# Gated cross-attention with two experts' stages: the first batch's front of the second attention is ordered ahead of the second batch's

## The chip, the cores and the metric

One Trainium2 chip, one core (core 0). The metric is device time in microseconds from the first to the last instruction of one execution, as the chip's clock counts it. Other cores are idle. TensorE, VectorE, ScalarE and GpSimd each run their own instruction stream in order; SyncE issues transfers (SP below), and 16 DMA engines carry them. Engines wait for each other by semaphores only.

## The reference, cut to what matters

Four stages add to a residual x of 8 batches x 256 tokens x 512: an attention with rotary positions, an expert stage, a second attention with normed queries and keys, and a routed stage of sparse maps. Only the second attention is touched:

```python
q = _ln((x @ Wq + bq).reshape(b, s1, H, HD), qn_w, qn_b)            # 16 heads of 32
kv = jnp.concatenate([y_main @ Wk + bk, y_main @ Wv + bv], axis=-1)
kv = kv.reshape(b, s2, H, 2 * HD)
k = _ln(kv[..., :HD], kn_w, kn_b)
v = kv[..., HD:]
ctx = _attn(qT, k.transpose(0, 2, 1, 3), v.transpose(0, 2, 1, 3))
ctx_dca = _attn(qT, k_dca.transpose(0, 2, 1, 3), v_dca.transpose(0, 2, 1, 3))  # last 16 rows
ctx = ctx + DCA_WEIGHT * ctx_dca
return ctx @ Wo + bo
```

Here `_ln` is a layer norm over the 32 columns of one head, with a weight and a bias, and x is itself layer-normed over its 512 columns before it comes in. The context y has 256 rows per batch, of which the last 16 have weights of their own and a softmax of their own.

## The kernel before, in words

`normed_attention` computes this stage. A batch is 256 tokens, two tiles of 128. Heads are worked in pairs: 8 pairs per batch, 64 steps in all. In step s, TensorE turns the exponentials of pair s (line 2221) and computes the scores of pair s + 2 (`scores`, line 2211); VectorE takes the maxima of pair s + 1 (`top`, 1925), ScalarE its exponentials (2039), GpSimd scales its last 16 columns (`second_scaled`, 1849 to 1853).

The front of a batch makes what the pairs need. It is a list of named items, and the table `ITEMS_AT` gives the step of each, counted from the batch's own first pair (batch b starts at step 8b): C turns the context, X0 and X1 turn the normed tokens, Q0, Q1, K1, K0 are the products whose results are normed per head, V1 and V0 the values. Each Q or K tile is evacuated by ScalarE into `cen` (2087), squared by GpSimd (`squares`, 1828), summed per head by VectorE (1951). When all four are summed, VectorE takes the inverse square roots of 64 sums per row in a chain of 13 small operations (`over_spread`, 1959 and 84 to 97; called the spread below). Then GpSimd norms the tile in three operations (`norm`, 1836, 1839, 1842), ScalarE makes the high part (2096), VectorE the low part (1966), and items q0a, q1a, k1a, k0a (first four pairs) and q0b, q1b, k1b, k0b (last four) turn them on TensorE (2145). ScalarE evacuates the units of tile 0, VectorE those of tile 1, both into `qT` and `kT`, and SP copies these into the layout of the scores, `q4` in 4 transfers and `k4` in 8 (`spread_out`, 1747 and 1752). Three PSUM banks `W` are used in turn by all items.

Other tables place the rest: `SQUARED_AT`, `SUMMED_AT`, `SPREAD`, `SCALED_AT`, `HIGH_AT`, `LOW_AT` and `TOKENS` (GpSimd applies the layer norm to x, 1820). Statistics of x: those of batch 0 and 1 are taken before the loop; those of batches 2 to 7 (12 tiles) at the steps of `STATS_AT` (2012), and at step `SCALES` a chain of 20 small operations turns them into scales (`layer_norm_scalars`, 113 to 127). GpSimd's tokens of batch 2 wait for that (`all_scales`).

Each engine walks the steps from `FIRST` to `LAST` and in each step issues what the tables name for every batch. So the fronts of batch 0 and batch 1 overlap before step 0: batch 0's items stand at steps -17 to 0, batch 1's at -9 to 8. DCA items D, E, F make the 16 rows once, and SP puts them into `cen` and V of each batch (`dca_keys` 1758, `dca_values` 1763).

## Time and profile before

| | us |
|---|---|
| median of 3 runs | 2203.88 |
| lowest, highest | 2186.25, 2235.4 |
| the profiled execution | 2186.77 |
| its span, first to last instruction | 2185.0 |
| TensorE busy in the span | 1893.5 |
| VectorE, ScalarE, GpSimd busy | 1127.2, 921.9, 1012.6 |

The rows of the trace that matter have a section of their own. A row of the timeline gives the start in us from the span's start, the length, the engine, the line of the program, the operation, output <- input, how many were merged, and in brackets the idle time of the engine before it and who ended that. The second attention begins near 1462 us; its pair loop ends near 1898 us.

### The profile page before, as it was taken

To read this page: it belongs to the slowest core of one execution; us is meant where nothing else is said; L and a number is where in the kernel's file an instruction comes from. 1 tells how busy PE (TensorE), PEld (TensorE's weight loads), DVE (VectorE), ACT (ScalarE), POOL (GpSimd) and SP (SyncE) were. 2 spreads that over 40 slices of the span, in tenths; PEclk is the share of its full clock that TensorE was granted. 3 is DMA by queue.
4 is the path that set the end of the run, shared out by engine and by line. 5 is a ranking of instruction groups with operands and counts; after the bars stand their busy time and mean duration, and the time that the engine had idled before them with its cause. 6 is when DMAs were issued, how large, how long until landed. Compare 5 with 4: busy or idle time off the path is not lost. (4 is left out here: it accounts for less than half of the span.)

```text
span 2185.0 us, 37999 instructions
## 1 busy us (share of the span) xinstructions
PE 1893.5 (87%) x11294; PEld 1380.0 (63%) x11294; DVE 1127.2 (52%) x2563; ACT 921.9 (42%) x2626; POOL 1012.6 (46%) x1058
## 2 busy tenths in 40 slices
PE   4689999999879999989999999966799999765992
PEld 1355666666549899978888899953565655422441
DVE  5567767777545763322332222226677778561114
ACT  3367777776633322222222222212566666432110
POOL 1478777877510542222333343424565454155540
PEclk9999999999889999999999999988899999977996
DMA  8588888787715663579778766432444444182446
GB/s 313 179 250 261 262 250 247 227 254 237 239 48 180 113 140 87 149 216 283 210 198 233 228 163 161 88 74 85 96 99 98 92 100 110 33 231 77 138 135 259
DMA packets 189404, 373.74 MB, mean 171 GB/s; under 512 B 47658, under 2 KB 89267, under 8 KB 183380
## 3 DMA queue, kind: packets, MB, share of 16 engines
q1 hardware_dynamic: 157596, 309.18, 46.6%
q0 software_dynamic: 31616, 62.14, 13.3%
q8 instruction: 104, 1.70, 0.3%
q14 instruction: 88, 0.72, 0.1%
HBM read 193.42 MB, written 135.33 MB: 150 GB/s over the span
## 5 line engine op out<-in xcount | busy, mean ns | idle before, releaser
L701 ACT ACTIVATE a_P<-a_SC,a_nm 128x256 f32<-128x256 f32 x512 | 235.9, 473 | 132.2 <-DVE a_nm L606 131.4
L1174 POOL DMA_INDIRECT b_y_rows<-b_ysb,b_entry x79 | 124.6, 1577 | 351.2 <-DMA b_y_rows<-b_ysb,b_entry 227.4
L606 DVE TENSOR_REDUCE a_nm<-a_SC 128x2 f32<-128x512 f32 x256 | 164.8, 685 | 142.4 <-PE a_SC L847 142.4
L1383 DVE TENSOR_TENSOR b_xl<-b_XT,b_xh 128x512 fp32r<-128x512 f32 x111 | 76.7, 691 | 250.0 <-ACT b_xh L1325 248.9
L569 POOL TENSOR_TENSOR a_praw<-a_praw,a_phigh 128x704 f32<-128x704 f32 (+2 forms) x126 | 191.2, 1517 | 10.3
L858 PEld LDWEIGHTS a_T<-ident,a_P 128*128 128x128 f32 x1024 | 119.2, 145 | 74.6 <-issue 39.7
L858 PE MATMUL a_T<-ident,a_P 128*128 128x128 f32 x1024 | 147.2, 283 | 21.5 <-DVE a_PT L618 20.6
L567 POOL CAST a_phigh<-a_praw 128x704 fp32r<-128x704 f32 (+2 forms) x126 | 112.7, 895 | 93.8 <-DMA a_praw<-in_L_ffn_wd 32.6
L1389 DVE TENSOR_TENSOR b_al<-b_AT,b_ah 128x384 fp32r<-128x384 f32 x111 | 61.8, 557 | 176.7 <-ACT b_ah L1330 176.7
L1320 ACT ACTIVATE b_ysb<-b_Y 128x512 f32<-128x512 f32 x79 | 47.3, 598 | 249.5 <-PE b_Y L1265 249.5
L2039 ACT ACTIVATE c_P<-c_SC,c_nm 128x240 f32<-128x240 f32 x256 | 115.7, 457 | 76.9 <-DVE c_P L1931 76.8
L1330 ACT ACTIVATE b_ah<-b_AT 128x384 fp32r<-128x384 f32 x111 | 54.6, 492 | 209.1 <-PE b_AT L1254 209.1
L2713 PE MATMUL d_Y<-d_Me,d_xT 128*128 x312 | 142.2, 599 | 0.0
L1233 PE MATMUL b_G<-b_wh,b_xh 128*128 (+2 forms) x444 | 101.9, 352 | 18.9 <-issue 10.5
L1325 ACT ACTIVATE b_xh<-b_XT 128x512 fp32r<-128x512 f32 x111 | 66.0, 595 | 124.0 <-PE b_XT L1204 124.0
L1157 POOL DMA_INDIRECT b_slots<-b_ent,b_at_u x64 | 63.9, 998 | 114.6 <-DVEq L1464 96.3
L1165 POOL DMA_INDIRECT b_xg<-b_xn_rows,b_entry x79 | 77.7, 983 | 68.5 <-PE b_XT L1204 41.0
L2916 DVE TENSOR_SCALAR d_ysb<-d_Y,d_entry 128x512 f32<-128x512 f32 x39 | 29.3, 751 | 145.5 <-PE d_Y L2713 145.5
L701 ACT ACTIVATION_READ_ACCUMULATOR a_P<-a_SC,a_nm 128x1 f32 x512 | 103.9, 203 | 0.0
L1925 DVE TENSOR_REDUCE c_nm<-c_SC 128x2 f32<-128x480 f32 x128 | 82.1, 641 | 39.6 <-PE c_SC L2211 39.2
L1245 PE MATMUL b_U<-b_wh,b_xh 128*128 (+1 forms) x444 | 99.2, 345 | 0.0
L1265 PE MATMUL b_Y<-b_wh,b_ah 128*128 (+1 forms) x333 | 95.6, 395 | 0.9 <-ACT b_ah L1330 0.9
(478 smaller groups left out, 4826.3 us busy)
## 6 DMA issues: line engine op xcount, KB each, us to landing
w_parts<-a_phigh SPq DMA_DIRECT2D x72, 352.0 KB, 3.5
w_parts<-a_praw SPq DMA_DIRECT2D x72, 352.0 KB, 4.2
b_wh<-w_parts SPq DMA_DIRECT2D x18, 1216.0 KB, 10.6
b_wl<-w_parts SPq DMA_DIRECT2D x18, 1216.0 KB, 13.6
c_q<-c_qT SPq DMA_DIRECT2D x64, 256.0 KB, 4.3
c_k<-c_kT SPq DMA_DIRECT2D x128, 128.0 KB
b_wh<-w_parts SPq DMA_DIRECT2D x18, 704.0 KB, 5.2
b_wl<-w_parts SPq DMA_DIRECT2D x18, 704.0 KB, 8.1
```

Source lines behind the costliest of these rows:

```text
L567: eng.tensor_copy(high[:, 0:k * m], raw[:, 0:k * m]).then_inc(phigh_done, 1)
L569: eng.tensor_tensor(raw[:, 0:k * m], raw[:, 0:k * m], r32(high[:, 0:k * m]), ALU.subtract).then_inc(plow_done, 1)
L606: eng.tensor_reduce(nm[:, g % 4, j, :], SC[j][:, :].rearrange("p (t k) -> p t k", t=BT), AX.X, ALU.max, negate=True).then_inc(topped, 1)
L701: e = eng.activation(Pr[:, i, t, :], SC[j][:, t * S:(t + 1) * S], ACT.Exp, bias=nm[:, g % 4, j, t:t + 1], accum_out=den[:, h, t:t + 1])
L858: m = eng.transpose(T_[j][:, k * S + t * P:k * S + (t + 1) * P], Pr[:, (2 * g + j) % NP_, t, k * P:(k + 1) * P], core.ident[:, :])
L1174: eng.indirect_dma_start(out=y_rows, out_offset=bass.IndirectOffsetOnAxis(ap=entry[:, r, 1:2].bitcast(U32), axis=0), in_=ysb[:, v % RING, ...
L1233: m = eng.matmul(G[v % 2][:, 0:n], x_[:, v % 2, k, :], gate_cols(w_, at_unit[v], k, n), start=(i == 0), stop=(i == 3 * KD - 1))
L1245: m = eng.matmul(U[:, 0:I], x_[:, v % 2, k, :], up_cols(w_, at_unit[v], k), start=(i == 0), stop=(i == 3 * KD - 1))
L1265: m = eng.matmul(Y[v % 2][:, :], a_[:, v % 2, j * P:(j + 1) * P], down_rows(w_, at_unit[v], j), start=(i == 0), stop=(i == 3 * J - 1))
L1925: eng.tensor_reduce(nm[:, g % 4, j, :, 0], v[:, :, 0:MAIN], AX.X, ALU.max, negate=True)
L2039: e = eng.activation(Pr[:, i, t, 0:MAIN], SC[j][:, t * S:t * S + MAIN], ACT.Exp, bias=nm[:, g % 4, j, t, 0:1], accum_out=den[:, h, t, 0:1])
L2713: m = eng.matmul(Y[r % 2][:, :], xT[:, r % 2, k, 0:P], Me[:, bass.ds(e, 1), k, :].rearrange("p o d -> p (o d)"), start=(k == 0), stop=(k = ...
```

## The change

Batch 0's front gets its own place in the order. A function `turn_of` maps a step to the place in the tables: for batch 0, steps -26 to -10 stand for places -20 to -4, steps -9 to -4 are empty, and from -3 on the places are as before. Batch 1 and all later batches keep theirs. The loop starts six steps earlier. So batch 0's items up to k0a and V1 stand ahead of all of batch 1's. The tiles of batch 0 are normed by VectorE (`first_norm`) and no longer by GpSimd. The statistics of batches 2 to 7 and their scalars move from steps -11 to -8 to steps -6 to -4. Half of the first keys' copies, j = 1, is issued by ScalarE (`second_keys`) and no longer by SP.

```diff
+    FRONT, FRONT_END = 6, -4
-    FIRST, LAST = -20, END + 5
+    FIRST, LAST = -20 - FRONT, END + 5
-    STATS_AT, SCALES = {-11: 4, -10: 8, -9: 12}, -8
+    STATS_AT, SCALES = {-6: 4, -5: 8, -4: 12}, -4
...
+    def turn_of(s, b):
+
+        if b:
+            return s - PAIRS * b
+        if s + FRONT <= FRONT_END:
+            return s + FRONT
+        return s if s > FRONT_END else None
...
-            at = s - PAIRS * b
+            at = turn_of(s, b)
...
-        return [(b, table[s - PAIRS * b]) for b in range(B) if s - PAIRS * b in table]
+        return [(b, table[turn_of(s, b)]) for b in range(B) if turn_of(s, b) in table]
...
-                for j in range(2):
+                for j in range(2 if (b, n, i) != (0, "k", 0) else 1):
...
                 for b, n in due(s, SCALED_AT):
-                    norm(b, n)
+                    if b:
+                        norm(b, n)
...
+            def first_norm(n):
+
+                x = cen[:, n, :].rearrange("p (h e) -> p h e", e=HD)
+                case = (0, 0, 2, 1)[n]
+                eng.wait_ge(sq_done, n + 1)
+                eng.tensor_tensor(x, x, lw[:, 0, n * H:(n + 1) * H].unsqueeze(2).to_broadcast([P, H, HD]),
+                                  ALU.mult).then_inc(vseq, c.inc())
+                eng.wait_ge(vseq, c.now)
+                eng.tensor_tensor(x, x, lnc[:, case, 0, :].unsqueeze(1).to_broadcast([P, H, HD]),
+                                  ALU.mult).then_inc(vseq, c.inc())
+                eng.wait_ge(vseq, c.now)
+                eng.tensor_tensor(x, x, lnc[:, case, 1, :].unsqueeze(1).to_broadcast([P, H, HD]),
+                                  ALU.add).then_inc(scaled, 1)
...
+                for b, n in due(s, SCALED_AT):
+                    if b == 0:
+                        first_norm(n)
...
+            def second_keys():
+
+                for t in range(BT):
+                    is_freed(eng, (0, f"k{t}a"))
+                for r in range(0, P, HD):
+                    src = R + (HD if r >= R else 0)
+                    eng.dma_start(r32(k4[r:r + HD, 1, 0:HALF, :]), r32(kT[src:src + HD, :, :])).then_inc(copied["k"], 16)
...
+                if (0, "k0a") in items(s):
+                    second_keys()
```

On TensorE, between batch 0's K0 product and the first scores. `c_ctx` and `c_xn` are turns of a batch's context and tokens, `c_xT` its Q products, `c_hlq` and `c_hlk` turns of normed tiles, `c_cT0` and `c_cT1` products on the context of batch 0 and 1. Before:

```order
L2145 MATMUL c_W1<-ident,c_ctx 128x128 x4
L2145 MATMUL c_W2<-ident,c_xn 128x128 x4
L2145 MATMUL c_W0<-ident,c_xn 128x128 x4
L2154 MATMUL c_W1<-X,c_xT 128x512 x4
L2157 MATMUL c_W1<-c_bias,c_flags 128x512
L2154 MATMUL c_W2<-X,c_xT 128x512 x4
L2157 MATMUL c_W2<-c_bias,c_flags 128x512
L2145 MATMUL c_W0<-ident,c_hlq 128x128 x4
L2145 MATMUL c_W1<-ident,c_hlq 128x128 x4
L2154 MATMUL c_W2<-X,c_cT1 128x512 x2
L2157 MATMUL c_W2<-c_bias,c_flags 128x512
```

Now:

```order
L2182 MATMUL c_W1<-ident,c_hlq 128x128 x4
L2182 MATMUL c_W2<-ident,c_hlq 128x128 x4
L2182 MATMUL c_W0<-ident,c_hlk 128x128 x4
L2182 MATMUL c_W1<-ident,c_hlk 128x128 x4
L2191 MATMUL c_W2<-X,c_cT0 128x512 x2
L2194 MATMUL c_W2<-c_bias,c_flags 128x512
L2182 MATMUL c_W0<-ident,c_ctx 128x128 x4
L2182 MATMUL c_W1<-ident,c_xn 128x128 x4
L2182 MATMUL c_W2<-ident,c_xn 128x128 x4
L2191 MATMUL c_W0<-X,c_xT 128x512 x4
L2194 MATMUL c_W0<-c_bias,c_flags 128x512
```

Batch 0's four normed tiles and its V1 come first, and batch 1's context, tokens and Q products behind them; the first scores still stand behind all of these.

On VectorE, between batch 0's last unit (`c_kT`) and batch 1's spread. Before:

```order
L1971 CAST c_kT<-c_W 128x4x128
L1951 TENSOR_REDUCE c_ss<-c_sq 128x16 x3
L1959 TENSOR_SCALAR c_ss<-c_ss 128x64
L87 TENSOR_SCALAR c_lw<-c_ss 128x64
L88 TENSOR_SCALAR c_lw<-c_ss 128x64
L90 TENSOR_SCALAR c_lw<-c_lw 128x64
```

Now:

```order
L1995 CAST c_kT<-c_W 128x4x128
L1961 TENSOR_REDUCE c_ss<-c_sq 128x16
L2039 BN_STATS c_st<-Xa 128x6 x4
L1961 TENSOR_REDUCE c_ss<-c_sq 128x16
L2039 BN_STATS c_st<-Xa 128x6 x4
L1961 TENSOR_REDUCE c_ss<-c_sq 128x16
L2039 BN_STATS c_st<-Xa 128x6 x4
L113 TENSOR_TENSOR c_llw<-c_st 128x12
L114 TENSOR_TENSOR c_llw<-c_st 128x12
```

The 12 statistics stand between batch 1's sums, and the scalar chain (`c_llw`, 20 operations) ahead of its fourth sum, which stands at the chain's end, followed by batch 1's spread. (Batch 0's three norm operations per tile stand on VectorE right behind batch 0's spread, where the statistics stood.)

On GpSimd, up to batch 1's first norm (`c_cen<-c_cen,c_lw`); `c_sq` are squares, `c_xn` tokens. Now:

```order
L1829 TENSOR_SCALAR c_xn<-Xa,c_lnsc 128x512 x2
L1837 TENSOR_TENSOR c_sq<-c_cen 128x512 x4
L1829 TENSOR_SCALAR c_xn<-Xa,c_lnsc 128x512 x2
L1837 TENSOR_TENSOR c_sq<-c_cen 128x512 x3
L1829 TENSOR_SCALAR c_xn<-Xa,c_lnsc 128x512 x2
L1837 TENSOR_TENSOR c_sq<-c_cen 128x512
L1845 TENSOR_TENSOR c_cen<-c_cen,c_lw 128x512
```

Batch 0's norms have gone, its four squares stand together, and the tokens of batch 2 stand ahead of batch 1's fourth square, as before.

## Rows read from the trace of the kernel before

**Rows 1.** Windows: length, busy of PE, PEld, DVE, ACT, POOL, clock, DMA share, GB/s.
```profile
1514.00:1532.00 18.00, 8.86 (x37) 4.81 (x35) 8.53 (x22) 4.48 (x8) 5.10 (x6) 0.93 0.57 137
1532.00:1545.00 13.00, 8.14 (x31) 5.97 (x32) 7.03 (x22) 6.36 (x16) 9.85 (x9) 0.76 0.35 81
1545.00:1560.00 15.00, 15.00 (x69) 9.66 (x68) 9.38 (x29) 10.95 (x37) 8.89 (x13) 0.95 0.31 70
```

**Rows 2.** Timeline of TensorE: start us, length us, line, operation [idle before <-releaser].
```profile
1486.11 1.88 PE L2154 MATMUL c_W<-X,c_cT 128*128 128x512 f32 x4
...
1503.30 6.55 PE L2154 MATMUL c_W<-X,c_xT 128*128 128x512 f32 x8 [9.70 <-ACT c_xT L2079]
...
1509.29 0.79 PE L2157 MATMUL c_W<-c_bias,c_flags 128*128 128x512 f32 x1
...
1509.92 3.60 PE L2154 MATMUL c_W<-X,c_xT 128*128 128x512 f32 x8
...
1532.19 1.19 PE L2211 MATMUL c_SC<-c_k,c_q 128*128 128x256 f32 x4 [7.86 <-DMA c_k<-c_kT]
...
1534.03 3.05 PE L2154 MATMUL c_W<-X,c_cT 128*128 128x512 f32 x4
...
1545.50 4.15 PE L2154 MATMUL c_W<-X,c_xT 128*128 128x512 f32 x8
```

**Rows 3.** Timeline of GpSimd, the first two batches' squares, norms and tokens.
```profile
1492.85 1.04 POOL L1828 TENSOR_TENSOR c_sq<-c_cen 128x512 f32<-128x512 f32 x1
...
1497.88 1.05 POOL L1836 TENSOR_TENSOR c_cen<-c_cen,c_lw 128x512 f32<-128x512 f32 x1 [3.99 <-DVEq L1962]
...
1506.89 1.59 POOL L1839 TENSOR_TENSOR c_cen<-c_cen,c_lnc 128x512 f32<-128x512 f32 x1
...
1512.29 1.27 POOL L1842 TENSOR_TENSOR c_cen<-c_cen,c_lnc 128x512 f32<-128x512 f32 x1
...
1527.14 1.04 POOL L1828 TENSOR_TENSOR c_sq<-c_cen 128x512 f32<-128x512 f32 x1 [11.59 <-DMA c_cen<-X]
...
1528.16 1.52 POOL L1820 TENSOR_SCALAR c_xn<-Xa,c_lnsc 128x512 f32<-128x512 f32 x2
```

**Rows 4.** Timeline of VectorE: scalar chains, statistics, last sum and spread.
```profile
1485.14 0.95 DVE L113 TENSOR_TENSOR c_llw<-c_st 128x2 f32<-128x2 f32 x1
...
1489.18 0.16 DVE L127 SCALAR_TENSOR_TENSOR c_lnsc<-c_llw 128x2 f32<-128x2 f32 x1
...
1497.89 4.85 DVE L2012 BATCH_NORM_STATS2 c_st<-Xa 128x6 f32<-128x512 f32 x8
...
1507.28 1.23 DVE L113 TENSOR_TENSOR c_llw<-c_st 128x12 f32<-128x12 f32 x1
...
1517.12 0.17 DVE L127 SCALAR_TENSOR_TENSOR c_lnsc<-c_llw 128x12 f32<-128x12 f32 x1
...
1530.72 0.69 DVE L1951 TENSOR_REDUCE c_ss<-c_sq 128x16 f32<-128x512 f32 x1 [1.82 <-POOL c_sq L1828]
...
1534.31 0.23 DVE L97 SCALAR_TENSOR_TENSOR c_lw<-c_lw 128x64 f32<-128x64 f32 x1
```

**Rows 5.** Timeline of the DMA queue that SyncE issues on.
```profile
1518.82 3.33 SPq L1747 DMA_DIRECT2D c_q<-c_qT  x4
...
1524.94 5.25 SPq L1752 DMA_DIRECT2D c_k<-c_kT  x8
```

**Rows 6.** Timeline of ScalarE: evacuation, first high part, first exponential.
```profile
1478.75 0.60 ACT L2087 ACTIVATE c_cen<-c_W 128x512 f32<-128x512 f32 x1 [4.06 <-PE c_W L2157]
...
1538.45 0.63 ACT L2096 ACTIVATE c_hlq<-c_cen 128x512 fp32r<-128x512 f32 x1 [10.96 <-POOL c_cen L1842]
...
1540.39 0.46 ACT L2039 ACTIVATE c_P<-c_SC,c_nm 128x240 f32<-128x240 f32 x1
```

**Rows 7.** One source line: operation, durations ns (min/median/max), first and last start.
```profile
L1523 DVE TENSOR_TENSOR X<-X,b_next_mean x8: 691/692/694, 1077.4 to 1126.7; 128x512 f32<-128x512 f32 x8
```

**Rows 8.** Timeline of TensorE, a wait inside the pair loop.
```profile
1581.38 1.97 PE L2221 MATMUL c_T<-ident,c_P 128*128 128x128 f32 x8 [5.88 <-POOL c_P L1853]
```

More of the change, by code:

```diff
@@ L1606, in items @@
         for b in range(B):
-            at = s - PAIRS * b
+            at = turn_of(s, b)
             named = ITEMS_AT.get(at, ()) if b < B - 1 or at < PAIRS else LAST_AT.get(at, ())
             found += [(b, n) for n in named]
-        found += [(0, n) for n in DCA_AT.get(s, ())]
+        found += [(0, n) for n in DCA_AT.get(turn_of(s, 0), ())]
         return [i for i in found if i[1][0] in "qk"] + [i for i in found if i[1][0] not in "qk"]
     def due(s, table):
-        return [(b, table[s - PAIRS * b]) for b in range(B) if s - PAIRS * b in table]
+        return [(b, table[turn_of(s, b)]) for b in range(B) if turn_of(s, b) in table]
     number = {}
@@ L1789, in _ @@
                 for b in range(B):
-                    if b and s - PAIRS * b == TOKENS:
+                    if b and turn_of(s, b) == TOKENS:
                         context(b)
@@ L1868, in _ @@
                 for b in range(B):
-                    if s - PAIRS * b == TOKENS:
+                    if turn_of(s, b) == TOKENS:
                         tokens(b)
                 for b, n in due(s, SCALED_AT):
-                    norm(b, n)
+                    if b:
+                        norm(b, n)
                 for b, n in due(s, SQUARED_AT):
@@ L2004, in _ @@
                 for b in range(B):
-                    if s - PAIRS * b == SPREAD:
+                    if turn_of(s, b) == SPREAD:
                         over_spread(b)
+                for b, n in due(s, SCALED_AT):
+                    if b == 0:
+                        first_norm(n)
                 for b, n in due(s, LOW_AT):
```

## The prediction

> **What bounds the kernel now.** I read in this order: the page, to find the stage; the table of windows, for who is busy there; the timelines of TensorE, GpSimd, VectorE, ScalarE and the DMA queue over the first 80 us of the second attention. The page puts no engine above 87%, and the last chain lies in the routed stage, which the change doesn't touch. So only the length of the second attention's start can move the end, and it moves it one for one if the loop behind it is bound by an engine. It is: from 1545 us on TensorE is busy 15.00 of 15.00 us, while in the two windows before it is busy 8.86 of 18 and 8.14 of 13 [rows 1]. The question is when the pair loop gets going.
>
> Two events start it. The first is the first score product, at 1532.19, after 7.86 us of waiting for the keys' copies [rows 2]. The keys are late since GpSimd norms the first batch's four tiles from 1497.88 to 1513.56 [rows 3], VectorE then finishes the scalars of the statistics at 1517.29 [rows 4], and one queue issues the q copies at 1518.82 and eight k copies from 1524.94 on [rows 5]. The second event is the end of the **second** batch's inverse square roots (the spread) on VectorE, at 1534.54 [rows 4]. It stands ahead of the first row maxima on that engine, and GpSimd's first norm of that batch, ScalarE's high part of it (1538.45) and only then the first exponential (1540.39) hang on it [rows 6]. The first exponential comes 5.85 us after the spread. Speeding up the keys is worth something only if this second event moves too.
>
> **The change, part by part.** Times are those of the profiled execution.
>
> *First batch's chain.* The square of its fourth tile goes ahead of the second batch's tokens on GpSimd; it started at 1492.85 [rows 3] and can start when the third square ends, about 1.5 us earlier. The spread, which ended at about 1497.9, ends at 1496.4. VectorE then does 12 operations. Their nearest row is a 128x512 tensor by broadcast operation of the same engine, 0.692 us [rows 7]; with 0.03 between dependent ones a tile takes 2.1 us, four 8.5 us, with the low parts between. The last low part ends at about 1508.0. GpSimd needed 15.7 us for the norms alone [rows 3]. Bound from above, if the broadcast of 32 columns costs VectorE what it costs GpSimd (1.27 in rows 3): 15 us, no gain. I take 8.5, by the engine's own row.
>
> *Copies.* q copies are issued from about 1507.6, and the k copies end around 1517 instead of 1532. Four of the eight k copies move to ScalarE. SP issues eight in 5.25 us [rows 5], so the four save SP 2.6 us and, at the same price, keep ScalarE 2.6 us, from about 1512.0 to 1514.6. No row shows ScalarE issuing; the ends are 0 and 2.6, and I take 2.6. What is queued behind it on ScalarE is the second batch's context and tokens, for whose turn its Q product on TensorE waits. The Trainium skill, "DMA: Bandwidth & Descriptors", section "Issuing engines are not separate DMA queues", says that a second issuing engine only saves the sequencer's issue time, all transfers running on the same 16 DMA engines; by that this edit is worth at most SP's issue time, which is no longer waited for.
>
> *What TensorE must still do first.* The order on TensorE puts the second batch's context, tokens, Q, Q, K, K behind the first batch's k0a and V1, and still ahead of the first scores. Before, all but the tail of these filled the time in which the norms ran. Now: k0a at 1508.1, V1 to 1510.7 at full clock or 1511.9 at the lower level (its matmuls take 1.88 us at one and 3.05 at the other [rows 2]), its evacuation 0.6, ScalarE's issue 2.6, context and first tokens 1.1: the first Q product starts at 1515.1 to 1516.3. At 1503.30, after 9.70 us idle, such a product with its bias took 6.8 us, the next one 3.6 to 3.8 [rows 2]. TensorE is idle most of 1492 to 1508 now, so I take 6.8. It ends (call this T) at **1522.5**, against 1510.1 before; between 1516.7 (no issue cost, full clock) and 1523.1. Then Q 3.65, K 2.0, K 2.0 and two transposes: the first scores could be ready at 1531.5, hardly earlier than 1532.19. The keys' gain of 15 us ends here, behind TensorE.
>
> *Statistics of the other batches.* The 12 statistics and their scalar chain left the first batch's norms and now stand on VectorE between the second batch's sums, each sum waiting for its square. From T: evacuation and square 1.8 (0.60 [rows 6] and 1.04 [rows 3] with gaps), sum 0.65, four statistics 2.46 (half of 4.85 [rows 4]); the second sum waits to T+5.45, +3.1 with its statistics; the third follows to T+11.7. The scalar chain of 20 operations took 4.2 us when GpSimd was quiet (1485.14 to 1489.34) and 10.0 us when GpSimd normed (1507.28 to 1517.29) [rows 4]; GpSimd waits here for exactly this chain, so I take 4.2. T+15.9. Then GpSimd's tokens of the third batch 1.52 and, behind them in its order, the second batch's fourth square 1.04 [rows 3]: T+18.6. Sum and spread take 3.8 (1530.72 to 1534.54 [rows 4]): **T+22.4**, so 1544.9 against 1534.5, **+10.4**. In the order before, that square waited only for a late DMA of 11.59 us [rows 3], and that wait goes; the new one takes its place.
>
> The Trainium skill, "SBUF — State Buffer", section "SBUF: two separate sides", says that VectorE and GpSimd share a port pair as an exclusive lock; by that the 10.0 us are blocking by the norms, and the chain is cheap in its new place. By the dearer row the sum would be 6 us more.
>
> *TensorE's clock behind it.* TensorE is now idle from about 1532 until the first exponential, at about 1550.7, but for a few transposes and one product. The product at 1545.50 took 4.15 us, after 9.70 us idle one took 6.55 [rows 2]: **+2**, between 0 and +3, on the path, since TensorE is what bounds from there.
>
> Removing GpSimd's 12 operations of the first batch, and its wait on the late DMA, gives nothing beyond this. The order of every engine from the first score on is as before, so the shift is carried to the end: 10.4 + 2 = **+12 us**, 2186.8 to **2199** for an execution like the profiled one. Bounds of the sum: T at 1516.7 and nothing for the clock give +4.6; the dear scalar chain, T at 1523.1 and +3 give +20. The runs shown have a median of 2203.88 (2186.25 to 2235.4); the profiled one, 2186.77, is near the lowest. Between it and the median lies 2195.3, my level for a fresh median of this kernel before; with +12 that is **2207**.
>
> **Rivals.**
> 1. *The keys were the bound* (9%). If the first scores set the pace and the second batch's front hides, the gain is what TensorE leaves: at T = 1516.7 the scores come at about 1526, 6 us earlier. For it: the 7.86 us wait. Against: the first maxima waited for the spread, not for scores. Time: 2189, or 2181 for an execution like the profiled one.
> 2. *The shift is absorbed* (8%): gaps of the loop, such as the 5.88 us in front of the transposes at 1581.38 [rows 8], swallow 10 us. Against: that gap belongs to the third batch's spread, which moves along. Time: 2195.
> 3. *The scalar chain costs 10 us in its new place*, and the clock 3 (18%): +19, 2214.
> 4. *Each batch pays* (3%), the one on the slow side: if the front of every later batch came late against its scores by what the second one does, the wait of 5.88 us [rows 8] would double in each of seven batches: 41 + 12, 2248, slower by over 2%. It decides once a later batch's spread ends after the maxima that follow it; the unchanged order from the first score on speaks against it.
> 5. *The change doesn't do what it says* (2%): VectorE's norms cost 15 us as on GpSimd; then T is 6 us later, +18, 2213.
>
> **How the numbers follow.** My forecast has 60%: +12, 2207. The median of a few executions moves by itself by some 8 us either way, as the runs show, and the sum's bounds are +5 and +20. From 2195.3 - 8 to 2203.9 + 20 is 2187 to 2224; reaching a little into rival 4 and the scatter above, 2187 to 2228. A measurement of this kernel tells about 2% (44 us) from no change. Only rival 4 and scatter pass it: slower 0.04, faster 0.03, within 2% 0.93.
>
> **What would show it.** In the changed kernel's timeline: the last low part of the first batch at about 1508 (the norms' term), first k copies before 1515, the second batch's first Q product ending near 1522 (else the issue cost or the clock was mis-sized), the statistics' scalar chain 4 us long and ending near T+16, the spread at about 1545, the first exponential 5.9 us behind it, and the routed stage starting 10 to 14 us later. Wrong if the spread ends before 1536, if ScalarE's four issues take no time, or if the first maxima wait for scores.

## The result, and the profile after

| | before | changed |
|---|---|---|
| median of 20 runs each, us | 2194.47 | 2204.56 |
| lowest, highest | 2179.77, 2235.4 | 2197.23, 2215.2 |
| the profiled execution | 2186.77 | 2198.5 |
| ratio changed / before | | 1.0051 [1.0035, 1.0066] |

Slower by 0.5%: 11 us, by the interval 8 to 14. That is within the 2% that I called no change, and the interval excludes no difference. Twelve executions on another chip gave 1.0055 [1.0026, 1.0084].

One shift has to be taken out before the timelines are compared. The first per-head sum of batch 0 (VectorE, `c_ss`) is the last event that both kernels reach by the same work. I call its start t0: 1489.48 before, 1493.37 changed, 3.89 us apart, though nothing ahead of it was changed. In traces of runs 1 to 4 below, with the same work ahead of it, it lay between 1486.6 and 1496.1. So every time below is told against t0, and a single execution's total says little about this change.

| from t0, us | before | changed | difference |
|---|---|---|---|
| batch 1's first Q product starts | 13.82 | 27.80 | +13.98 |
| first scores | 42.71 | 39.92 | -2.79 |
| batch 1's spread ends | 45.06 | 53.44 | +8.38 |
| first exponential | 50.91 | 59.28 | +8.37 |
| last output product but one | 408.55 | 418.94 | +10.39 |
| first product of the routed stage | 421.93 | 430.62 | +8.69 |

The last row is read from these two, before and changed:

```profile
1911.41 0.41 PE L2720 MATMUL d_R<-ident,d_raw 8*128 8x8 f32 x4 [4.09 <-DMA d_raw<-in_L_ffn_gate_w]
```

```profile
1923.99 0.59 PE L2757 MATMUL d_R<-ident,d_raw 8*128 8x8 f32 x4 [4.09 <-DMA d_raw<-in_L_ffn_gate_w]
```

It is 1.7 us less than the row above it, since the last output product but one took 5.40 us in the trace of the kernel before and 3.70 us in the changed one's.

The first scores came earlier, and the first exponential later, with the spread. TensorE of the changed kernel (start, length, operation, [idle before <-releaser]):

```profile
1507.55 1.12 PE L2182 MATMUL c_W<-ident,c_hlq 128*128 128x128 f32 x4 [13.47 <-DVE c_hlq L1990]
...
1513.61 3.51 PE L2191 MATMUL c_W<-X,c_cT 128*128 128x512 f32 x4
...
1521.17 3.70 PE L2191 MATMUL c_W<-X,c_xT 128*128 128x512 f32 x8 [2.41 <-ACT c_xT L2106]
1524.30 0.79 PE L2194 MATMUL c_W<-c_bias,c_flags 128*128 128x512 f32 x1
...
1533.29 0.72 PE L2248 MATMUL c_SC<-c_k,c_q 128*128 128x256 f32 x4
...
1547.87 1.09 PE L2182 MATMUL c_W<-ident,c_ctx 128*128 128x128 f32 x4 [11.47 <-DVE c_qT L1995]
```

The norms on VectorE let the first turn start at 1507.55, but batch 1's Q product starts only at 1521.17, where [rows 2] had it at 1503.30. The 7.86 us that the first scores waited for keys in [rows 2] have gone: there is no idle bracket at 1533.29. In their place stand 11.47 us of idleness at 1547.87. VectorE says where that comes from; first the norms, then what stands between batch 1's sums:

```profile
1500.63 0.69 DVE L1979 TENSOR_TENSOR c_cen<-c_cen,c_lw 128x512 f32<-128x512 f32 x1
...
1511.96 0.68 DVE L1990 TENSOR_TENSOR c_hlk<-c_cen,c_hlk 128x512 f32<-128x512 f32 x1
...
1526.89 0.69 DVE L1961 TENSOR_REDUCE c_ss<-c_sq 128x16 f32<-128x512 f32 x1 [13.64 <-POOL c_sq L1837]
1527.49 2.46 DVE L2039 BATCH_NORM_STATS2 c_st<-Xa 128x6 f32<-128x512 f32 x4
1530.55 0.69 DVE L1961 TENSOR_REDUCE c_ss<-c_sq 128x16 f32<-128x512 f32 x1 [0.59 <-POOL c_sq L1837]
1531.15 2.46 DVE L2039 BATCH_NORM_STATS2 c_st<-Xa 128x6 f32<-128x512 f32 x4
1533.53 0.67 DVE L1961 TENSOR_REDUCE c_ss<-c_sq 128x16 f32<-128x512 f32 x1
1534.11 2.46 DVE L2039 BATCH_NORM_STATS2 c_st<-Xa 128x6 f32<-128x512 f32 x4
1536.61 0.18 DVE L113 TENSOR_TENSOR c_llw<-c_st 128x12 f32<-128x12 f32 x1
...
1540.04 0.17 DVE L127 SCALAR_TENSOR_TENSOR c_lnsc<-c_llw 128x12 f32<-128x12 f32 x1
1542.99 0.69 DVE L1961 TENSOR_REDUCE c_ss<-c_sq 128x16 f32<-128x512 f32 x1 [2.79 <-POOL c_sq L1837]
...
1546.58 0.23 DVE L97 SCALAR_TENSOR_TENSOR c_lw<-c_lw 128x64 f32<-128x64 f32 x1
```

The sum at 1526.89 waited 13.64 us for the first square of batch 1. The statistics that [rows 4] had beside GpSimd's norms (1497.89) now stand in three pieces of 2.46 us between the sums. The scalar chain runs from 1536.61 to 1540.21. Only then come the fourth sum, 1542.99, and the spread, which ends at 1546.81. GpSimd's side of the same stretch:

```profile
1531.42 1.04 POOL L1837 TENSOR_TENSOR c_sq<-c_cen 128x512 f32<-128x512 f32 x1 [0.91 <-ACT c_cen L2114]
1540.44 1.52 POOL L1829 TENSOR_SCALAR c_xn<-Xa,c_lnsc 128x512 f32<-128x512 f32 x2 [7.97 <-DVEq L2044]
1541.92 1.04 POOL L1837 TENSOR_TENSOR c_sq<-c_cen 128x512 f32<-128x512 f32 x1
```

The square of the fourth tile stands behind the third batch's tokens, which wait 7.97 us for the scalars. ScalarE had evacuated that tile at 1533.29, so it lay ready for 8.6 us. In the order before, the transfer was late: the third square waited 11.59 us for it [rows 3], and the tokens and the fourth square stood behind. Here the third square waits 0.91 us, for ScalarE (row 1531.42), and the fourth for VectorE's scalars. ScalarE and SP:

```profile
1517.38 0.60 ACT L2143 ACTIVATE c_V<-c_W 112x512 f32<-112x512 f32 x1 [2.94 <-PE c_W L2194]
1517.45 2.53 ACTq L2137 DMA_DIRECT2D c_k<-c_kT  x4
1520.03 0.60 ACT L2089 ACTIVATE c_cT<-c_W 128x512 f32<-128x512 f32 x1 [2.05 <-issue]
...
1550.71 0.63 ACT L2123 ACTIVATE c_hlq<-c_cen 128x512 fp32r<-128x512 f32 x1 [16.64 <-POOL c_cen L1851]
...
1552.65 0.46 ACT L2066 ACTIVATE c_P<-c_SC,c_nm 128x240 f32<-128x240 f32 x1
```

```profile
1512.13 3.23 SPq L1756 DMA_DIRECT2D c_q<-c_qT  x4
1515.46 3.54 SPq L1761 DMA_DIRECT2D c_k<-c_kT  x4
```

ScalarE's four issues (ACTq) take 2.53 us, and ScalarE's evacuation of the context turn behind them starts at 1520.03, with "issue" as what it waited for. SP's eight k copies of [rows 5] have become four. The three windows of [rows 1], not shifted (length, busy of PE, PEld, DVE, ACT, POOL, clock, DMA share, GB/s):

```profile
1514.00:1532.00 18.00, 15.59 (x45) 7.57 (x43) 4.52 (x8) 4.41 (x8) 2.65 (x3) 0.92 0.56 128
1532.00:1545.00 13.00, 4.39 (x23) 2.72 (x22) 9.48 (x35) 1.20 (x2) 2.99 (x4) 0.84 0.00 0
1545.00:1560.00 15.00, 6.87 (x23) 5.06 (x24) 8.25 (x25) 8.64 (x26) 12.51 (x12) 0.50 0.30 70
```

TensorE's work has been moved into the first window (15.59 us instead of 8.86). The second and third are nearly empty of it, with a granted clock of 0.84 and 0.50. The loop that filled [rows 1]'s last window has not begun.

### The profile page after: what moved, and what is told of

It is laid out like the page before. It is cut to its first block and busy times, and to the rows that moved or that the text cites. A ratio compares the mean times of both kernels' runs of the same rounds, so it can differ in the third digit from the quotient of the medians.

```text
span 2196.8 us, 37996 instructions
## 1 busy us (share of the span) xinstructions
PE 1896.8 (86%) x11294; PEld 1384.8 (63%) x11294; DVE 1130.2 (51%) x2575; ACT 921.2 (42%) x2626; POOL 997.6 (45%) x1046
## 5 line engine op out<-in xcount | busy, mean ns | idle before, releaser
L1174 POOL DMA_INDIRECT b_y_rows<-b_ysb,b_entry x79 | 124.5, 1576 | 348.4 <-DMA b_y_rows<-b_ysb,b_entry 223.8
L1165 POOL DMA_INDIRECT b_xg<-b_xn_rows,b_entry x79 | 77.8, 985 | 68.5 <-PE b_XT L1204 47.1
L847 PE MATMUL a_SC<-a_kT,a_qT 32*128 32x256 f32 x512 | 83.2, 338 | 15.8 <-DMA a_qS<-a_qT 5.5
```

Of the source, the lines that this page charges most:

```text
L847: m = eng.matmul(SC[j][:, t * S:(t + 1) * S], q[r:r + R, p // 2, t * P:(t + 1) * P], kT[r:r + R, p // 2, :], start=(half == 0), stop=(half ...
L1174: eng.indirect_dma_start(out=y_rows, out_offset=bass.IndirectOffsetOnAxis(ap=entry[:, r, 1:2].bitcast(U32), axis=0), in_=ysb[:, v % RING, ...
```

## The experiments

Every run lists A, the time from t0 to the first exponential, and S, the end of batch 1's spread from t0. The changed kernel gave A 59.28, and in a second profile (called the repeat below) 60.37: there batch 1's first Q product took 5.40 us instead of 3.70. Runs are compared with that in mind. The ratio is to the kernel before on the same chip. A and S are read from one trace each.

**1. Statistics early (stats_early): is it the statistics that hold the spread?**

```diff
-    STATS_AT, SCALES = {-6: 4, -5: 8, -4: 12}, -4
+    STATS_AT, SCALES = {-9: 4, -8: 8, -7: 12}, -7
```

> The changed kernel with the 12 statistics and their scalar chain moved ahead of the second batch's sums (steps -9 to -7), into VectorE's idle time of 13.6 us. Let A be the time from batch 0's first head sum to the first exponential (50.9 us before, 59.3 changed). Theory 1 (the statistics between the sums make batch 1's spread late): the fourth square follows the K0 product at once, A falls to 50.8, the kernel is 8 to 10 us faster than the changed one. Rival (the first scores or the norms set the pace): the wait moves to the scores, A stays above 57.

Measured: ratio 1.0003 [0.998, 1.0026]. S 46.58, A 52.41, with the Q product at 5.40 us; against the repeat, which had it at 5.40 too, A is 7.96 us shorter. I had expected 50.8; the slower Q product accounts for 1.1 us of the 1.6 missing, if it costs here what it costs the changed kernel. The scalar chain's end and the four sums on VectorE:

```profile
1520.68 0.17 DVE L127 SCALAR_TENSOR_TENSOR c_lnsc<-c_llw 128x12 f32<-128x12 f32 x1
1524.89 0.69 DVE L1961 TENSOR_REDUCE c_ss<-c_sq 128x16 f32<-128x512 f32 x1 [4.04 <-POOL c_sq L1837]
1528.55 0.69 DVE L1961 TENSOR_REDUCE c_ss<-c_sq 128x16 f32<-128x512 f32 x1 [2.98 <-POOL c_sq L1837]
1530.50 0.69 DVE L1961 TENSOR_REDUCE c_ss<-c_sq 128x16 f32<-128x512 f32 x1 [1.26 <-POOL c_sq L1837]
1533.01 0.69 DVE L1961 TENSOR_REDUCE c_ss<-c_sq 128x16 f32<-128x512 f32 x1 [1.82 <-POOL c_sq L1837]
```

The chain is over 4 us before the first sum, and each sum waits for its square only. Moving one row of a table to earlier steps (still one or two behind those of the kernel before) takes away the slowdown. This is the cause of most of the result.

**2. The kernel before with late statistics (before_stats_late): does the same edit alone do harm without the rest?**

```diff
-    STATS_AT, SCALES = {-11: 4, -10: 8, -9: 12}, -8
+    STATS_AT, SCALES = {-6: 4, -5: 8, -4: 12}, -4
```

> The kernel before with only the statistics moved to steps -6 to -4, as the change has them. The scalar chain no longer stands in front of the first keys' low parts, so the keys' copies land about 4 us earlier. Theory 1 (batch 1's spread sets the first exponential): A rises from 50.9 to about 55, although the keys are earlier. Rival (the keys set it): A falls to about 47.

Measured: one time, 2198.34. The first scores came 2.94 us earlier (39.77 from t0 against 42.71), and still A rose by 2.19 to 53.10, with S 47.26. That the keys get faster and the first exponential gets later in one and the same trace rules out the keys as what bounds the start. The scalar chain took 3.60 us (1533.11 to 1536.71), and the fourth sum waited 2.79 us for its square behind it, as in the changed kernel. I had expected 55: the third square still waited 6.72 us for its transfer here, so the first two pieces of statistics stood in time in which VectorE would have been idle anyway.

**3. Norms of batch 0 back on GpSimd (norms_gpsimd)**

```diff
                 for b, n in due(s, SCALED_AT):
-                    if b:
-                        norm(b, n)
+                    norm(b, n)
...
-                for b, n in due(s, SCALED_AT):
-                    if b == 0:
-                        first_norm(n)
```

> The changed kernel with batch 0's norms back on GpSimd. Theory 1: the norms take 14.8 to 15.7 us and not 8.9, the turns of k0a and with them batch 1's first Q product are 4 to 5 us later, A rises from 59.3 to 63.5 to 64.4. Rival (the engine of the norms is hidden, the second front's TensorE work being the bound anyway): A stays at 59.3.

Measured: one time, 2195.82, with t0 at 1486.60. A 63.91, 4.63 us more than the changed kernel: in this order the keys' chain leads to batch 1's Q product and through it to the spread, so VectorE's norms earn 4.6 us. The time reads lower than the changed kernel's only because t0 lies 6.8 us earlier in this execution.

**4. All first keys from one queue (keys_one_queue)**

```diff
-                for j in range(2 if (b, n, i) != (0, "k", 0) else 1):
+                for j in range(2):
...
-                if (0, "k0a") in items(s):
-                    second_keys()
```

> The changed kernel with all eight first key copies issued by SP. Theory 1 (ScalarE's four issues hold up batch 1's context and tokens): the wait of 2.41 us in front of batch 1's first Q product shrinks to about 0.4, A falls by 2.0 to 57.3. Rival (the issue is hidden behind the V1 evacuation or the keys become late): A stays at 59.3 or rises.

Measured: one time, 2199.35. The Q product starts 2.75 us earlier, and A is 2.76 shorter, 56.52. The queue and TensorE's first scores:

```profile
1518.16 6.83 SPq L1761 DMA_DIRECT2D c_k<-c_kT  x8
```

```profile
1520.84 3.70 PE L2189 MATMUL c_W<-X,c_xT 128*128 128x512 f32 x8 [0.26 <-ACT c_xT L2106]
...
1532.96 0.72 PE L2246 MATMUL c_SC<-c_k,c_q 128*128 128x256 f32 x4
```

Eight issues by SP end at 1524.99, 8 us ahead of scores that wait for nothing. The second queue buys nothing here, and costs 2.76 us on the path, for ScalarE's 2.53 us of issuing. By the Trainium skill, "DMA: Bandwidth & Descriptors", section "Issuing engines are not separate DMA queues", a second issuing engine saves no more than the time to initiate the transfers. The trace agrees: SP's issues shrank from 6.83 us to 3.54, nobody waited for that, and ScalarE took the other part over. The page also calls that time usually small relative to the DMA itself; here it was 2.76 us of the path, since ScalarE issued between two links of a chain.

**5. The kernel before with one transfer moved (before_row_first).** In [rows 3] the third square, that of the key tile with the 16 DCA rows, waited 11.59 us for a DMA: the DCA keys that SP issues into `cen` behind the q copies. The tokens and the fourth square, whose row in the kernel before is this one, stood behind it:

```profile
1529.65 1.04 POOL L1828 TENSOR_TENSOR c_sq<-c_cen 128x512 f32<-128x512 f32 x1
```

The edit puts the transfer ahead of the q copies:

```diff
+                if s < 0:
+                    for b, n in items(s):
+                        if n == "K1":
+                            dca_keys(b)
                 for b, n in items(s):
-                    if n == "K1":
+                    if n == "K1" and s >= 0:
                         dca_keys(b)
```

> The kernel before with one change: ahead of the loop's first pair, SP puts batch 1's 16 DCA rows into its key tile before batch 0's q copies and not behind them. Theory 1 (before too, batch 1's spread set the first exponential, through the square that waited 11.59 us for this transfer): the spread ends about 5 us earlier, A falls from 50.9 to about 46, although the keys' copies are no earlier. Rival (the keys set the first exponential before): A stays at 50.9 or rises by the 0.6 us that the copies are issued later.

Measured: ratio 0.9977 [0.9951, 1.0002]. S 38.05, 7.0 us earlier, A 44.05, 6.9 earlier; I had expected 46. Now the third square waits 4.61 us, and the first maxima wait 4.08 us for the scores:

```profile
1559.56 1.04 POOL L1832 TENSOR_TENSOR c_sq<-c_cen 128x512 f32<-128x512 f32 x1 [4.61 <-DMA c_cen<-X]
```

```profile
1566.73 0.23 DVE L97 SCALAR_TENSOR_TENSOR c_lw<-c_lw 128x64 f32<-128x64 f32 x1
...
1571.95 0.66 DVE L1929 TENSOR_REDUCE c_nm<-c_SC 128x2 f32<-128x480 f32 x1 [4.08 <-PE c_SC L2215]
```

So in the kernel before, a transfer's place in the queue set the spread. The first exponential still follows the spread by 6.0 us, against 5.9 before: the keys have drawn level with it and cost some 0.15 us, and a start earlier than this one needs both to move.

**6, 7. Two mixtures.** `mix` is the order of before with VectorE's norms, the DCA row first, and the statistics at -7, -6, -5. `combo` is the changed kernel with the edits of 1 and 4, and batch 0's V1 moved behind:

```diff
-            found += [(b, n) for n in named]
+            found += [(b, n) for n in named if (b, n) != (0, "V1")]
+            if (b, s) == (0, -3):
+                found.append((0, "V1"))
```

> The order of the kernel before (batch 1's front between batch 0's), with VectorE norming batch 0's tiles, the DCA rows' transfer ahead of the q copies, and the statistics at steps -7, -6 and -5 in VectorE's gaps. Theory 1: ScalarE's first high part comes 3 us earlier and lets batch 1's context and tokens through, batch 1's spread ends at 39 after the first sum, A falls to 45, some 6 us (0.3%) faster than the kernel before. Rival (the gain of VectorE's norms always ends behind TensorE's products): A stays at 50 or above.

> The changed kernel with three edits: statistics at steps -9 to -7, all first key copies from SP, and batch 0's V1 product moved from ahead of batch 1's front to behind it. Theory 1: batch 1's first Q product starts at 21.5 after the first sum (27.8 changed, 25.05 with one queue), the spread ends near 41, A is 47, about 12 us faster than the changed kernel and 4 faster than before. Rival (what is taken from in front of the Q product comes back as a wait elsewhere, such as the keys' copies or the colder TensorE): A 50 or more.

Measured: mix 0.9983 [0.9958, 1.0008], S 41.25, A 47.10. combo 0.9983 [0.9961, 1.0006], S 40.85, A 46.69. combo came where it was forecast (47), mix 2.1 us short of its 45. Both take the changed kernel's loss away, and neither can be told from the kernel before. combo also prices one part: the changed kernel's A of 59.28 less 6.87 (run 1) and 2.76 (run 4) is 49.65, so V1 behind batch 1's front gave about 3.0 us more, if the three edits add up.

**8. Fourth square ahead of the third batch's tokens (square_first)**

```diff
+                if s < 0:
+                    for b, n in due(s, SQUARED_AT):
+                        squares(b, n)
                 for b in range(B):
...
-                for b, n in due(s, SQUARED_AT):
-                    squares(b, n)
+                if s >= 0:
+                    for b, n in due(s, SQUARED_AT):
+                        squares(b, n)
```

> The changed kernel with batch 1's fourth square ahead of batch 2's tokens on GpSimd. Theory 1 puts the statistics and their scalars, 8 of the 8.4 us, in VectorE's order, and only 2.7 in GpSimd's: A falls from 59.3 to 56.5. Rival (the square behind the tokens, which wait for the scales, is the whole of it): A falls to 51.

Measured: one time, 2235.48, on the chip of runs 5 to 7, where the kernel before has a median of 2225.02. S 52.43, A 58.27, with the Q product at 5.40 us; against the repeat that is 2.1 us less, where I had put 2.7. The rival's 51 is far off.

```profile
1565.26 1.04 POOL L1837 TENSOR_TENSOR c_sq<-c_cen 128x512 f32<-128x512 f32 x1 [0.91 <-ACT c_cen L2118]
1567.20 1.04 POOL L1837 TENSOR_TENSOR c_sq<-c_cen 128x512 f32<-128x512 f32 x1 [0.91 <-ACT c_cen L2118]
1574.27 1.53 POOL L1829 TENSOR_SCALAR c_xn<-Xa,c_lnsc 128x512 f32<-128x512 f32 x2 [6.03 <-DVEq L2048]
```

The square now runs at 1567.20, and the tokens wait for the scalars alone. But the sum that takes it stands behind the statistics and the scalar chain on VectorE. The tokens' place costs what GpSimd's order adds, some 2 us; VectorE's order is the larger part, as run 1 shows.

**9. All that pays, on the order before (best).** To `mix` come run 8's edit and the statistics of the later batches between the first pairs:

```diff
-    STATS_AT, SCALES = {-7: 4, -6: 8, -5: 12}, -5
+    STATS_AT = {-7: (4, 6), 0: (6, 9), 1: (9, 12), 2: (12, 14), 3: (14, 16)}
+    SCALES = {-7: (4, 6), 3: (6, 16)}
...
-                    eng.wait_ge(all_scales, min(b, 2))
+                    eng.wait_ge(all_scales, min(b, 3))
```

> The kernel mix with the statistics split: batch 2's two tiles and their scalars at step -7, the other ten tiles at steps 0 to 3 and their scalars at step 3 (batch 3's tokens wait for them), and ahead of the first pair the squares of a step stand before its tokens on GpSimd. Theory 1 (batch 1's spread minus what stands in its chain, then the scores): the spread ends near 36 after the first sum (41.3 in mix, 45.1 before), the first scores at 37 to 39 become the later event, A is 41 (40 to 43), and the kernel is 8 to 10 us (0.4%) faster than before. Rival (the ten statistics in the loop cost TensorE what they gave): A falls, but the loop behind it is 5 us or more longer than any seen (over 370 from the first exponential to the start of the second but last output product), and the time is that of mix.

Measured: ratio 0.9989 [0.9964, 1.0015]. S 34.50, A 40.99: 9.9 us less than the kernel before, as meant. The time doesn't follow: 9.9 us would be a ratio of 0.9955, outside the interval. The rival's sign, a loop of over 370 us, didn't show either; it took 363.9. This row of TensorE shows the first part of why:

```profile
1593.88 0.66 PE L2248 MATMUL c_T<-ident,c_P 128*128 128x128 f32 x4 [4.40 <-POOL c_P L1858]
```

**10, 12. Does TensorE's idleness cost the loop anything (warm, warm2)?** Turns of the identity into the idle bank O fill the gaps ahead of the third batch's items: 70 ahead of C in `warm`; 98, 10 and 34 ahead of C, X0 and X1 in `warm2`.

```diff
                 if n == "C":
+                    if b == 2:
+                        for _ in range(98):
+                            eng.transpose(O[:, 0:P], core.ident[:, :], core.ident[:, :])
...
+                if b == 2 and n[0] == "X":
+                    for _ in range((10, 34)[int(n[1])]):
+                        eng.transpose(O[:, 0:P], core.ident[:, :], core.ident[:, :])
```

> The changed kernel with 70 extra turns of the identity into an idle PSUM bank, ahead of batch 2's context, where TensorE stood idle 11.47 us. They fill about 9.8 us at full clock. Theory 1 (part of the loss, 1 to 3 us, is TensorE at its lower level behind that gap): A stays at 59, batch 2's first Q product takes 3.6 to 3.7 and not 5.3, the loop starts 1.5 to 2 us earlier, and the kernel is about 2 us faster than the changed one. Rival (the clock behind the gap costs nothing, or the extra turns delay the context): no difference or slower.

> The changed kernel, with 98 turns of the identity ahead of the third batch's context turns, 10 ahead of its first and 34 ahead of its second token turns, all into the idle output bank. They fill the 11.47, 1.29 and 3.98 us in which TensorE waits before the first exponential (0.111 us per turn, by the run with 70 of them), and add no wait. Clock theory (TensorE's idleness there costs 1.6 us at the start of the loop): the third batch's first Q product takes 3.6 to 3.7 us instead of 5.27, and the next score product behind it comes 1.6 us earlier against the first exponential; the first exponential stays 59.3 us (to 60.4) behind the first head sum; the ratio to the kernel before is 1.0055 less 0.0007, which five rounds cannot tell from 1.0055. Rival (the level of that product does not hang on the idleness in front of it): it takes 5.3 us all the same.

Measured: warm 1.0063 [1.0042, 1.0083], A 59.34; waits of 3.86, 1.29 and 3.98 us were left, and the third batch's first Q product took 5.27 us as before. That run did not test the question. warm2 did: 1.0031 [1.0009, 1.0053], A 60.45. Its filled gaps, and the changed kernel's product:

```profile
1567.74 10.86 PE L2205 MATMUL c_O<-ident 128*128 128x128 f32 x98
1579.38 0.63 PE L2182 MATMUL c_W<-ident,c_ctx 128*128 128x128 f32 x4 [0.78 <-DVE c_qT L1995]
1579.84 1.25 PE L2210 MATMUL c_O<-ident 128*128 128x128 f32 x10
1581.75 0.63 PE L2182 MATMUL c_W<-ident,c_xn 128*128 128x128 f32 x4 [0.65 <-DVE c_kT L1995]
1582.21 3.88 PE L2210 MATMUL c_O<-ident 128*128 128x128 f32 x34
1586.83 0.63 PE L2182 MATMUL c_W<-ident,c_xn 128*128 128x128 f32 x4 [0.74 <-ACT c_V L2143]
...
1588.21 3.60 PE L2191 MATMUL c_W<-X,c_xT 128*128 128x512 f32 x8
```

```profile
1557.89 5.27 PE L2191 MATMUL c_W<-X,c_xT 128*128 128x512 f32 x8
...
1594.48 1.97 PE L2258 MATMUL c_T<-ident,c_P 128*128 128x128 f32 x8 [5.87 <-POOL c_P L1862]
```

Between 1564 and 1590 no wait is longer than 0.78 us, the granted clock is 1.00 from 1564 to 1600, and the product takes 3.60 us. In time this can't be told: the ratio's interval holds the changed kernel's 1.0051 and 1.0055. The table below has what the trace says.

**11. The changed kernel again (after_again)**, unchanged.

> The changed kernel once more, beside the other kernels of this group. Theory 1: A is 59.3 within 1.2 (it depends on the clock of one Q product), time 1.004 to 1.006 of before. A rival by which the profiled pair of traces differed by chance would give an A near 51.

Measured: ratio 1.0055 [1.0026, 1.0084], S 54.53, A 60.37. Its V1 and its first Q product of batch 1 (3.51 and 3.70 us in the first trace):

```profile
1541.42 2.10 PE L2191 MATMUL c_W<-X,c_cT 128*128 128x512 f32 x4
...
1548.38 5.40 PE L2191 MATMUL c_W<-X,c_xT 128*128 128x512 f32 x8 [3.22 <-ACT c_xT L2106]
```

The granted clock was 0.57 during V1 and 1.00 during the Q product in the first trace, 0.89 (V1 with the turns behind it) and 0.69 here. So the lower level fell on the one or on the other.

**How much of a shift the loop keeps.** From the traces: the start of each batch's first output product (TensorE, `c_W<-X,c_aT`) and of the routed stage's first product (`d_R<-ident,d_raw`), counted from the first exponential. The last column is the routed stage's start from t0, less that of the kernel before.

| | A | batch 0 | batch 1 | batch 4 | batch 6 | last product but one | routed stage | shift from t0 |
|---|---|---|---|---|---|---|---|---|
| before | 50.91 | 76.9 | 123.0 | 262.8 | 340.4 | 357.6 | 371.0 | |
| changed | 59.28 | 78.0 | 124.5 | 264.8 | 342.4 | 359.7 | 371.3 | +8.7 |
| the repeat | 60.37 | 77.7 | 124.3 | 264.7 | 342.8 | 361.6 | 373.3 | +11.8 |
| warm | 59.34 | 78.0 | 124.6 | 264.9 | 342.4 | 359.6 | 371.3 | +8.8 |
| warm2 | 60.45 | 76.9 | 123.4 | 263.6 | 341.2 | 359.3 | 371.0 | +9.5 |
| norms_gpsimd | 63.91 | 77.9 | 124.1 | 264.1 | 341.5 | 358.8 | 370.5 | +12.4 |
| square_first | 58.27 | 79.4 | 125.9 | 266.5 | 345.6 | 364.5 | 376.4 | +12.8 |
| keys_one_queue | 56.52 | 79.1 | 125.6 | 265.8 | 343.2 | 360.4 | 372.1 | +6.7 |
| before_stats_late | 53.10 | 78.5 | 124.6 | 264.4 | 344.2 | 362.6 | 374.3 | +5.5 |
| stats_early | 52.41 | 77.8 | 124.3 | 264.4 | 341.8 | 359.1 | 371.1 | +1.6 |
| combo | 46.69 | 76.9 | 123.5 | 264.0 | 341.4 | 358.6 | 372.0 | -3.2 |
| mix | 47.10 | 79.5 | 126.0 | 266.2 | 345.8 | 364.6 | 376.3 | +1.5 |
| before_row_first | 44.05 | 78.7 | 124.8 | 265.0 | 344.8 | 363.3 | 375.0 | -2.9 |
| best | 40.99 | 82.9 | 129.1 | 268.7 | 346.6 | 363.9 | 375.5 | -5.4 |

The loop is not of one length: up to the routed stage it spans 370.5 to 376.4 us. Whether it starts early or late doesn't sort these: square_first starts 7.4 us later than the kernel before and its loop is the longest, combo starts 4.2 us earlier and its loop adds only 1.0 us. And the kernel before stands in its single trace near the short end, so that every comparison with it looks like a loss. Some of it can be read. Of best's 9.9 us, 6.0 are gone by batch 0's output product: the scalar chain of ten tiles in step 3 holds VectorE from 1588.07 to 1592.49, the first batch's weights on GpSimd wait behind it, TensorE waits 4.40 us for those (row 1593.88 above), and its granted clock is 0.66 in the 10 us behind that wait. before_row_first loses 1.8 us in batch 0 and 3.5 more behind batch 4, mix 2.6 and then 4.4 by the last product but one. What lengthens these loops behind batch 4 is open.

The timed ratios are the better witness. If the loop kept the whole of the earlier start, they would be 0.9969 for before_row_first, 0.9983 for mix and 0.9981 for combo; measured were 0.9977, 0.9983 and 0.9983, with intervals that hold these values and 1 as well. So for these three it is not shown that anything is lost, nor that anything is gained. Only best falls short of its 0.9955 by more than its interval (0.9964 to 1.0015).

## Why the prediction was right, point by point

The forecast was 2207 with +12 for a like execution; the median is 2204.56, and the ratio makes it +11. (The median of the kernel before is 2194.47 where I took 2195.3.) The times against t0, moved to the clock of the trace before (the changed kernel's less 3.89):

| step | predicted | measured |
|---|---|---|
| last low part of batch 0 ends | 1508.0 | 1508.8 |
| ScalarE's four issues | 2.6 us | 2.53 us |
| batch 1's first Q product starts | 1515.1 to 1516.3 | 1517.3 |
| that product, with its bias | 6.8 us | 3.9 us |
| T, its end | 1522.5 | 1521.2 |
| first scores ready | 1531.5 | 1529.4 |
| scalar chain | 4.2 us | 3.6 us |
| from T to the spread | 22.4 us | 21.7 us |
| spread ends | 1544.9 (+10.4) | 1542.9 (+8.4) |
| spread to first exponential | 5.85 us | 5.84 us |
| clock (measured up to batch 0's output product) | +2 | +0.8 to +1.1 |
| to the last output product but one | +12.4 | +10.4 |
| routed stage starts later by | 10 to 14 | 8.7, repeat 11.8 |

In the raw timelines the routed stage starts 12.6 us later, as forecast, but 3.9 of that is t0; against t0 the first pair of traces misses the 10 to 14, and the repeat meets it.

**The mechanism held.** The spread of the second batch, not the keys, starts the loop; the first exponential follows it by the same 5.8 us in both kernels. Runs 1 and 2 show it from both sides. Rival 1 (keys were the bound) is refuted by run 2: keys 2.9 us earlier, start 2.2 us later. Rival 2 (absorbed) is refuted by the routed stage's +8.7 and +11.8 and by the ratio. Rival 3 (10 us for the scalar chain in its new place) is refuted by 3.6 us. Rival 4 (each batch pays) is refuted by the wait of [rows 8], 5.87 us at 1594.48 where it was 5.88, and by the table: from batch 1's output to the last product but one the changed kernel's loop adds 0.6 us in all, where this rival had 41. Rival 5 (VectorE's norms cost 15 us) is refuted by 0.69 us an operation, the price of [rows 7].

**One reading was wrong.** The prediction says that the fourth square waited 11.59 us for a late DMA. It was the third one (run 5); the fourth ran at 1529.65, behind it and the tokens. The sum isn't changed by that, as both hung on the transfer.

**The Q product was mis-sized** by 2.9 us, partly made up by V1 ahead of it: V1 took 3.51 us at a granted clock of 0.57, and the matmuls behind it had 1.00. I had taken 6.8 us for a product behind idleness; I did not count what V1 and the turns between the idleness and it would do. The sum also lacked the 0.9 us between the start of k0a's turn and V1, and T came within 1.3 us since this and the product err in opposite ways. In other traces with the same order on TensorE ahead of it the product took 5.40 us (runs 8, 11 and 12, and run 1), so 3.70 is one of two cases. In the repeat V1 took 2.10 us instead, and the first exponential came 1.1 us later. By the repeat the spread is +9.5.

**The clock's +2 is not confirmed.** Up to batch 0's output product the changed kernel loses 1.1 us against the kernel before (78.0 against 76.9), the repeat 0.8; with the gaps filled (warm2) it is 0.0. The product itself gives back 1.67 us (5.27 against 3.60). That the 0.8 to 1.1 are this idleness rests on the one trace of warm2, and combo has 76.9 too, without any filling, with waits of 1.75, 1.74 and 4.00 us there and 4.55 us for the product. Up to the routed stage the loop adds 0.3 us in the changed kernel and 2.3 in the repeat. Both lie within the term's range of 0 to +3; the differences between loops in the table are as large, so its size stays open.

**The parts, priced by the runs** in A: VectorE's norms -4.6 (run 3), ScalarE's issues +2.8 (run 4), the late statistics +8.0 (run 1 against the repeat; against the changed kernel itself +6.9). Like with like (8.0 with the repeat's 9.5, or 6.9 with 8.4), 3.4 us are left for batch 0's items standing ahead of batch 1's, worked out as the remainder and not measured alone; combo's 3.0 us for V1 suggest that V1 is most of it. In my sum these were one path and not shares, so it got the total right without saying which part to undo. The Trainium skill, "SBUF — State Buffer", section "SBUF: two separate sides", says that the port pair which VectorE and GpSimd share is an exclusive lock; by that the scalar chain should be cheap where GpSimd waits. The traces agree: 3.6 us here, 3.60 in run 2, against 10.0 beside GpSimd's norms in [rows 4].

**Luck in the total.** The profiled execution of the changed kernel read 2198.5 where I said 2199. Of the 11.7 us between the profiled executions, 3.9 came from ahead of t0, where nothing was changed, 8.7 from the second attention, and 0.8 came back behind it. The ratio is the fairer test: my +12.4 lies within its 8 to 14 us, but near its upper end.

## What to carry to other kernels

Before speeding up the chain that a wait points to, look for the second chain that meets it, and ask which of the two is last: here 7.9 us of waiting for keys hid a spread that came 2.3 us behind them. Work that "only has to be done sometime" (statistics of later batches) belongs where its engine waits for something else, not between operations that each wait for one another; three numbers of a table were worth 7 to 8 us. And before building on a start won, ask whether it can be measured: four kernels that started the loop 4 to 10 us earlier (0.2 to 0.4% of the time) have intervals that reach 1, and three of these hold the full gain too. A single trace can't settle it either, since the loop behind the start differed by up to 6 us between traces.

## What the runs showed of the hardware

- DMA issues cost ScalarE about what they cost SP: 2.53 us for four, 0.63 each, and its next evacuation waited 2.05 us for them. SP's eight took 5.25 us before and 6.83 in run 4, 0.66 and 0.85 each, and its four in the changed kernel 3.54, 0.89 each.
- The same order gives two lengths of one product by the granted level: 3.70 or 5.40 us for batch 1's first Q product, with nothing changed ahead of it; V1 before it took 2.64 to 3.54 us where the Q product took 3.70 (the changed kernel's first trace, runs 3, 4 and 10), and 2.10 to 2.44 us where it took 5.40 (the repeat, runs 1, 8 and 12). A stretch compared by single traces needs its TensorE rows looked at first.
- A chain of 20 operations on 128x12 takes 3.6 us on a quiet VectorE and took 10.0 beside GpSimd's norms. Twelve 128x512 operations of VectorE with broadcast operands took 0.68 to 0.69 us each, while GpSimd took 1.05 to 1.76 for the same ones in the kernel before.
- t0 moved by up to 9.5 us between executions on one chip (1486.6 to 1496.1, runs 1 to 4) with unchanged work ahead of it, and lay at 1520 to 1529 in the traces of the other runs, on other chips.
